# A depthwise convolution and FFN kernel on one core: convolution units shifted by one image, band matrices built in thirds

## The reference

```python
x = x + _L0_conv_ref(_ln_c(x), L0_conv_kernel)      # 3x3 depthwise conv of LN(x), plus LN(x)
t = _to_tokens(x)
t = t + _L0_ffn_ref(_ln_t(t), W1, b1, W2, b2)       # 96 -> 384, relu, -> 96
```

## Time and profile before

| | us |
|---|---|
| median of three runs | 3327.44 (3323.74 to 3328.04) |
| the profiled execution: its time | 3330.84 |
| its span in the trace | 3329.1 |
| DVE busy | 3208.0 (96%) |
| ACT busy | 3100.2 (93%) |
| PE busy | 3009.6 (90%) |
| POOL busy | 1921.5 (58%) |
| mean granted clock of PE | 0.977 |

### The profile page before, as it was taken

The page is one execution under the profiler, slowest core; times in us unless marked ns, Lnnn a source line. Parts: engine busy times, 40 slices in busy tenths (PEclk is TensorE's granted clock), DMA queues, the critical chain, the costliest instruction groups (busy, mean ns, idle before and its releaser), DMA issues.

```text
span 3329.1 us, 78227 instructions
## 1 busy us (share of the span) xinstructions
PE 3009.6 (90%) x24902; PEld 2494.2 (75%) x24902; DVE 3208.0 (96%) x11767; ACT 3100.2 (93%) x7072; POOL 1921.5 (58%) x913
## 2 busy tenths in 40 slices
PE   5689999999999999999999999999999999999877
PEld 5677777777777777777777777777777777778744
DVE  8559999999999999999999999999999999999998
ACT  7679999999999999999999999999999999986766
POOL 0015666666666666666666666666666666666676
PEclk9999999999999999999999999999999999999966
DMA  7777777777777777777777777777777777766533
GB/s 224 212 204 213 223 226 223 223 228 223 227 224 224 223 226 226 222 227 223 225 224 224 228 222 227 221 226 222 225 228 221 228 222 227 223 202 180 159 117 100
DMA packets 277435, 713.58 MB, mean 214 GB/s; under 512 B 35001, under 2 KB 35106, under 8 KB 277026
## 3 DMA queue, kind: packets, MB, share of 16 engines
q1 hardware_dynamic: 271394, 694.12, 71.9%
q10 hardware_dynamic: 5632, 14.45, 1.3%
HBM read 539.84 MB, written 168.59 MB: 213 GB/s over the span
## 4 chain that ended last, share of the span: by engine, by line
DVE 75%; issue 12%; PE 8%; ACT 3%; DMA 2%; DVEq 1%; SPq 0%; POOLq 0%; ACTq 0%
DVE stats L650 25%; DVE xq L687 22%; DVE hid L640 13%; DVE images L699 6%; PE conv_ps L430 5%; DVE xt_ps L674 2%; DVE hid L645 2%; ACT images L522 2%; DVE rstd L678 1%; PE hid_ps L393 1%; DVE neg_mean L682 1%; PE y_ps L408 1%; DVE y L667 1%; ACT hid L501 1%; DMA band_ring<-bands 1%
## 5 line engine op out<-in xcount | busy, mean ns | idle before, releaser
L430 PE MATMUL conv_ps<-images,band_ring 112*112 112x222 f32 (+1 forms) x8928 | 1874.3, 354 | 31.5 <-DMA band_ring<-bands 31.5
L430 PEld LDWEIGHTS conv_ps<-images,band_ring 112*112 112x112 f32 x8928 | 1547.3, 177 | 178.5 <-issue 29.5
L275 POOL TENSOR_TENSOR xf<-xf,y 112x768 f32<-112x768 f32 x448 | 952.8, 2127 | 1149.2 <-DVE y L667 1149.2
L501 ACT ACTIVATE hid<-hid_ps 128x896 f16<-128x896 f32 x1344 | 1183.8, 918 | 82.0 <-PE hid_ps L393 82.0
L270 POOL TENSOR_TENSOR xf<-xf,images 112x768 f32<-112x768 f32 x448 | 981.5, 2191 | 254.3 <-ACT images L533 241.2
L522 ACT ACTIVATE images<-xn,neg_mean,rstd 112x96 f32<-112x96 f32 x2590 | 1040.6, 545 | 22.3 <-DVE neg_mean L682 17.8
L408 PEld LDWEIGHTS y_ps<-w2t,hid 128*128 128x128 f16 x10752 | 571.7, 100 | 399.0 <-ACT hid L501 208.5
L408 PE MATMUL y_ps<-w2t,hid 128*128 128x96 f16 x10752 | 671.9, 210 | 196.9 <-ACT hid L501 174.0
L687 DVE SCALAR_TENSOR_TENSOR xq<-xf,stats,xt_ps 112x96 fp8e5<-112x96 f32 x3584 | 840.8, 311 | 0.0
L393 PE MATMUL hid_ps<-xt,w1t 96*128 96x448 fp8e5 x2688 | 681.5, 363 | 22.1 <-ACT xt L493 22.1
L640 DVE TENSOR_SCALAR hid<-hid,b1q 128x896 f16<-128x896 f16 x1344 | 587.3, 466 | 14.3 <-ACT hid L501 13.9
(11 more groups left out here) (54 smaller groups left out, 753.1 us busy)
## 6 DMA issues: line engine op xcount, KB each, us to landing
band_ring<-bands SPq DMA_DIRECT2D x744, 294.0 KB, 5.3
xf<-in_x SPq DMA_DIRECT2D x462, 336.0 KB, 5.2
out<-xf SPq DMA_DIRECT2D x448, 336.0 KB, 4.0
xn<-in_x SPq DMA_DIRECT2D x434, 336.0 KB, 3.3
bands<-images ACTq DMA_DIRECT2D x16, 882.0 KB, 7.9
xf<-bands SPq DMA_DIRECT2D x24, 294.0 KB, 4.4
xf<-in_L_ffn_W SPq DMA_DIRECT2D x2, 144.0 KB, 2.8
xf<-in_L_conv_kernel SPq DMA_DIRECT2D x3, 3.4 KB
```

The costliest lines, as they stand in the source:

```text
L275: pool.tensor_tensor(res, res, y[:, e % 2], ALU.add).then_inc(summed, CW)
L430: mm = pe.matmul(dst[:, :, lo:hi], band_place(t < CONV_AT + UNIT, n)[:, PAIR * dx + i, :], images[:, m % 2, :, ch, lo + dx - 1:hi + dx - 1 ...
L501: nc.scalar.activation(hid[:, e % 2, TOK * j:TOK * (j + 1)].rearrange("p (u n) -> p u n", u=2), hid_ps[:, k, :, 0:HALF * H], ACT.Identity) ...
```

## The change

The units are shifted by one image. Unit 0 is image 0 alone, units 1 to 15 are images 1 and 2, 3 and 4 and so on, and unit 16 is image 31 alone. The first unit's convolution starts 14 steps earlier and the last ends 14 steps later: -43 to -16, then -15 to 12, and the last 405 to 432. A unit of one image moves 112 columns instead of 224 in each matmul, with the same weight loads. The bands are built in thirds of 16 groups, six builds of 384 columns a step instead of five of 288, 84 builds instead of 112. Two thirds stay in their staging place while unit 0 reads them as weights from there; the last third is read from DRAM into the ring of three, as all bands are from unit 1 on. All three thirds are sent to DRAM, in sends of 1176 KB. For the first 42 chunks the load, the statistics, the root, invert and negate are a step earlier than before, while normalise stays; the four places for loads serve those 42. On ACT the builds and sends stand behind the norm instead of ahead of it. The waits of the first FFN matmul stand at that matmul, each for what it needs. DVE's statistics wait for DVE's normalise alone, and invert waits for ACT's. The unused outer loop (`r`, `c`) is gone, which changes no instruction.

```diff
-        QUARTERS = 4
-        STAGED_AT = {UNIT: (0, 2), UNIT + CHUNKS: (1, 3)}
+        THIRDS = 3
+        STAGES = [(1, 1), (0, 0), (1, 0)]
+        BUILT = (2, 0, 1)
+        STAGED_AT = {CHUNKS: 2, 2 * CHUNKS: 0, 3 * CHUNKS: 1}
...
-        STEP_SETUPS = 5
+        SEND_AT = {2: (4, 1), 0: (14, 2), 1: (22, 2)}
+        STEP_SETUPS = 6
...
-        CONV_AT = -UNIT - 1
+        CONV_AT = -UNIT - 1 - CHUNKS
+        UNITS = B // IMGS + 1
+        FIRST_NORMS = UNIT + CHUNKS
...
+        def unit_images(t):
+            m = (t - CONV_AT) // UNIT
+            return slice(1, IMGS) if m == 0 else slice(0, 1) if m == UNITS - 1 else slice(0, IMGS)
...
-            return (e // UNIT) % 2, e // CHUNKS % IMGS, slice(CW * k, CW * k + CW)
+            return (e + CHUNKS) // UNIT % 2, (e // CHUNKS + 1) % IMGS, slice(CW * k, CW * k + CW)
...
+        def early(t, lag):
+            late, soon = t + lag + LOOP, t + lag + LOOP + 1
+            return [n for n in (late, soon) if 0 <= n < TOTAL and (n == soon) == (n < FIRST_NORMS)]
...
+        LOADED_FROM = 2 * TGROUPS
+        def bands_at(n):
+            if n < LOADED_FROM:
+                return band_stage(n // TGROUPS)[:, n % TGROUPS]
+            return band_ring[:, (n - LOADED_FROM) % BAND_RING]
...
                 def load_bands(t):
                     for ch in conv_channels(t):
+                        n = GROUPS * ((t - CONV_AT) // UNIT) + ch // PAIR
+                        if ch % PAIR == 0 and n >= LOADED_FROM:
...
+                            if n >= LOADED_FROM + BAND_RING:
+                                sp.wait_ge(conv_mm, n - BAND_RING + 1)
...
                 def ffn1(e, j):
                     k = (J * e + j) % 2
+                    if j == 0:
+                        wait(pe, xt_copied, e + 1)
+                    wait(pe, hid_cast, J * e + j - 1)
...
                 def statistics_c(n):
-                    for s in normed:
-                        wait(dve, s, LOOP * r + n - 1)
+                    wait(dve, normed[1], n - 1)
...
                 def invert_c(n):
                     wait(dve, std_c_done, n + 1)
+                    wait(dve, normed[0], n - 1)
...
                 def normalise(n, lo, hi):
...
+                        if n in STAGED_AT:
+                            act.wait_ge(bands_out[STAGED_AT[n]], 16 * SENDS)
+                            if n > CHUNKS:
+                                act.wait_ge(conv_mm, TGROUPS * (STAGED_AT[n] + 1))
```

More of the change, by code:

```diff
@@ L141, in metaformer @@
         band_col = [sem("band_col_dve"), sem("band_col_act")]
-        bands_out = [sem(f"bands_out{i}") for i in range(QUARTERS)]
+        bands_out = [sem(f"bands_out{i}") for i in range(THIRDS)]
         xn_in = [sem(f"xn_in{i}") for i in range(FIRST_NORM_RING)]
@@ L212, in band_place @@
[L212 to L224, removed]
@@ L227, in setups, with band_arrival @@
+        def band_arrival(n):
+            return band_in[(n - LOADED_FROM) % BAND_RING], dma_count(n - LOADED_FROM, BAND_RING)
+        def setups(t):
             n = STEP_SETUPS * (t - NORM_AT)
-            return range(n, min(n + STEP_SETUPS, QUARTERS * SETUPS)) if c == t and n >= 0 else range(0)
+            return range(n, min(n + STEP_SETUPS, THIRDS * SETUPS)) if n >= 0 else range(0)
         def run(eng, step):
-            for c in range(NORM_AT - 1, LOOP_AT):
-                step(0, c, c)
@@ L233, in run @@
[L233 to L238, removed]
+            for t in range(NORM_AT - 2, END):
+                step(t)
         with nc.Block() as block:
@@ L311, in load_xn, with load_bands @@
+                def load_xn(n):
                     for s in normed:
-                        wait(sp, s, norm_place_free(r, n))
-                    sp.dma_start(norm_place(n), chunk_of(x, r, n)).then_inc(norm_arrival(r, n)[0], 16)
-                def load_bands(r, c, t):
+                        wait(sp, s, norm_place_free(n))
+                    sp.dma_start(norm_place(n), chunk_of(x, n)).then_inc(norm_arrival(n)[0], 16)
+                def load_bands(t):
                     for ch in conv_channels(t):
[L317 to L325, removed]
@@ L333, in step @@
+                def step(t):
+                    for n in early(t, 3):
+                        load_xn(n)
                     if ffn_in(t + 3):
-                        wait(sp, x_out[(c + 3) % FFN_RING], dma_count(r, c + 3 - FFN_RING, FFN_RING))
+                        wait(sp, x_out[(t + 3) % FFN_RING], dma_count(t + 3 - FFN_RING, FFN_RING))
                     if ffn_in(t - 3):
-                        store(r, c - 3)
+                        store(t - 3)
                     if ffn_in(t + 3):
-                        load_xf(r, c + 3)
@@ L395, in ffn1, with ffn2 @@
                     mm.then_inc(hid_mm, 1)
-                def ffn2(r, e, u, at_last=None):
-                    n = 2 * (LOOP * r + e) + u
+                def ffn2(e, u):
+                    n = 2 * (e) + u
                     if u == 0:
-                        wait(pe, hid_quant, LOOP * r + e + 1)
+                        wait(pe, hid_quant, e + 1)
                     wait(pe, y_cast, n)
@@ L551, in step @@
                         if n % 2:
                             build(n)
-                    for q in range(QUARTERS):
-                        k = t - NORM_AT - (SETUPS * (q + 1) - 1) // STEP_SETUPS
-                        if c == t and 0 <= k < SENDS:
-                            send(q, k)
-                    if ffn_in(t - 3):
-                        cast_y(r, c - 3, 1)
-                    if ffn_in(t - 1):
-                        copy_xt(r, c - 1)
-                    if norm_in(t + 1):
-                        normalise(r, c + 1 + LOOP, 0, ACT_COLS // 2)
@@ L575, in step @@
-                    if norm_in(t + 2):
-                        root_c(r, c + 2 + LOOP)
-                    if ffn_in(t - 1):
-                        cast_hid(r, c - 1, 1)
-                        cast_hid(r, c - 1, 2)
+                    for third, (at, every) in SEND_AT.items():
+                        k, off = divmod(t - NORM_AT - at, every)
+                        if 0 <= k < SENDS and off == 0:
+                            send(third, k)
+                    if ffn_in(t - 1):
+                        cast_hid(t - 1, 1)
+                        cast_hid(t - 1, 2)
```

352 lines of the change are left out of this document (167 added, 185 removed).

## The result

The changed kernel takes 3300.01 us (median, 3299.31 to 3302.68) against 3327.03 (four executions of each kernel): a ratio of 0.9921, 95% interval 0.9909 to 0.9934. Its profiled execution took 3300.27 us for a span of 3298.5, 30.6 less than before. One execution of `e10_sends_bunched` took 5024.64 us at a mean granted clock of 0.56, the others of that kernel 3296.51 to 3303.83; it is left out of that kernel's ratio.

The account below looks back on a forecast made before the run. DVE was taken to bound the steady steps and FFN alone, PE convolution with FFN. Tail 13.3 us plus head 7.2 gave 20.5, steady steps nothing: 3307 us against a median of 3327.44, range 3286 to 3335.

Parts of the forecast that it names:

- The half-width pair: PE's weight load and matmul with 112 moving columns: 94 ns, against 188 at full width; the range keeps 177.
- that rival: The float32 weight load paces the half convolution at 177 ns a pair: 3328 us, no change; chance 0.08.
- The tail: Steps from 391 on: 14 at 6.35 us, 28 half-width at 5.95, 18 FFN alone at 5.86; gain 13.3 us.
- The steady steps: Steps -1 to 390: same instructions before and after, 6.94 us each, so no gain taken.
- The head: Steps -57 to -2 and the way into the steady steps: mostly an exchange of step lengths, gain 7.2 us.
- The builds' stage: Steps -57 to -44, norms and builds: DVE sets them at 3.65 us a step; step -43 begins at 72 us.
- The 4 us for late loads: Steps -57 to -44: added for loads landing late beside sends, a step of lead lost, and the slow start.
- Steps -43 to -30: Norm and half convolution with sends: loads set 3.1 us a step, 43.4 us, plus 2 for PE's lower clock.
- the 3.7 of the ring: Steps -25 to -16, third loaded from DRAM: three band places and SP's order make 3.7 us a step.
- The clock: PE's granted clock, expected to stay up in the half-width tail, with PE 74% busy in columns.
- the sign "0.5 between steps 405 and 432": Half-width tail: the prediction is wrong if the clock shows 0.5 between these steps.
- The rival: Clock falls in the half-width tail: 32 us lost there, some 8 in the head, 3347 us; chance 0.12.

Follow-up runs that it names:

- e10_sends_bunched: Changed kernel with only the send times altered, second and third send one a step from step -49 on, bands still read in place: 3298.07 us, ratio 0.9918.
- The first experiment: Kernel before, with only the waits of the first FFN matmul moved to where the change has them: 3319.16 us, ratio 0.9971.
- the second: Changed kernel with the waits of the first FFN matmul put back ahead of the last matmul of what stands before: 3308.45 us, ratio 0.9943.

## Why the prediction was right, step by step

*The sum*: 20.5 us forecast; 27.0 by the medians, 30.6 between the profiled executions. Of these 30.6 the head has 14.7 (7.2 forecast), the 385 steady steps 1.8 (nothing forecast), the tail 12.7 (13.3 forecast), and 1.4 stand between these stretches and at the end. The tail is right in its terms; the head is right in direction, forecast at half its size, and in places right by luck.

*The half-width pair*: 94 ns forecast, 98 measured. The float32 load's record of 177 ns was no pace; that rival is refuted. 98 lies at the builds' 97 for loads of as many columns, so the weight load, not the moving columns, may set it. That wasn't taken apart.

*The tail*: 13.3 us forecast. From the scale of step 391 to that of step 447 it is 336.9 instead of 349.6, 12.7. Its terms: 5.92 against 5.95 for the half steps; 6.48 against 6.35 for the fourteen, since I gave the moved wait its whole 0.32 us of the earlier trace rows and it returned 0.2.

*The steady steps*: taken at nothing, 1.8 us in 385 steps. The first experiment has the same 1.8, and the second takes 2.5 back, so it is the moved waits.

*The head*: 7.2 us forecast, 14.7 measured; this is the term that was mis-sized. Step by step:

- The builds' stage ended as forecast (71.7 against 72), by luck. The 3.17 us of the earlier trace rows were read as a step with 2.5 copies, but the step shown there has three; the steps with two copies are as long because DVE waits 0.2 to 0.3 us for ACT's root in them. With three, the same sum gives 3.17 - 1.08 + 1.38 = 3.47 us, and without the early step it is 3.48. The change has 3.65, because the early statistics wait for DVE's own normalise, which I hadn't named. The two errors met. The 4 us for late loads measured 3.7.
- Steps -43 to -30 took 42.2 us against 43.4 and 2 for the clock. The 2 us for a lower clock at the start had no row of the kernel before; the pace up to 76.1 us shows 2.5. But the reason I gave for the length, that the loads set it, is wrong: DVE waits only 4.1 of 42 us for loads there, and without the early step, with the loads' lead a step longer, the stage took the same 42.2. Its length was luck.
- Steps -29 to -26 took 12.0 us against 11, the one guess that was too short. Steps -25 to -16 took 34.4 against 37, or 3.44 each against the 3.7 of the ring, and -15 to -2 took 62.8 against 64.4, or 4.49 against 4.6.
- From there to the scale of step 2 it was 22.4 us against 23.

That the norm's loop over two places sets the steps with the full-width convolution is shown in the kernel before, where four places alone took 10 us off 28 steps; in the change four places brought 3.96 a step, with one column less on ACT. I listed the shorter lead of the loads as a cost of 4 us and did not see that the whole early step was a loss, of some 10 us.

*In place*: the prediction had no term of its own for it. It turned out to be worth some 30 us, twice the head's whole gain, and without it the change would have been no faster than before (3332).

*The clock*: 1.00 through the half-width convolution of the tail, with PE busy 41 of 50 us. It fell at 3195.9 us, 4 us after the last matmul of that convolution, while DVE was in step 432, so the sign "0.5 between steps 405 and 432" is met by the letter, but no half-width step was slowed. The rival is refuted. In the head the clock fell four times (below); I had put 1.5 us there.

## What to carry to other kernels

Work costs what the engine that sets its stage is charged: the same matmul columns cost 13 us in the tail and 20 in the head, by the medians. Prefetching earlier with as many buffers did not make loads safer here: each load still had to wait for its place and was needed a step sooner. An operation moved ahead of its old place can find itself behind a wait of its own engine. Count both before calling such a move free. Where one queue issues for two consumers with waits in order, a late consumer holds the other. And when a step length is taken from a row, count what is in that very step, not what is in a mean one.

## What was not expected of the hardware

The granted clock fell to 0.50 four times in the head, at 103.4, 141.0, 199.0 and 233.2 us, 3.4 us each. The first and the third fell in stages with PE busy 82% and 92% of the time. Rows of the third, columns as in the earlier trace rows:

```profile
195.60:199.00 3.40, 1.67 (x10) 1.43 (x9) 2.05 (x8) 2.04 (x7) 0.00 (x0) 1.00 0.96 260
199.00:202.40 3.40, 3.40 (x11) 2.86 (x10) 1.15 (x4) 2.08 (x6) 0.00 (x0) 0.50 0.36 80
```

In the 3.4 us ahead of the four falls PE had been busy 1.54, 1.41, 1.67 and 0.80 us, and the fall came when it was full again. Ahead of the third it had waited 1.73 us for a band; at the low clock its full-width matmuls then start 373 ns apart instead of 188, so some 9 pairs cost 1.7 us more, and the wait cost PE about twice its length. The variant with a full-width head, where PE is the fuller engine, has no fall between 76 and 3200 us. A mean share over a stage did not tell whether the clock holds; each fall stood behind a stall inside it (PE's longest waits there: 2.2 us for ACT's save, 1.4, 1.7 and 3.6 for a band). Over four falls that is at most some 7 us of PE's work. What they cost the kernel was not measured, and it may be less: the variant with the full-width tail has the same head and five falls, at other times, and its scale of step 2 starts 1.5 us earlier.
